# Loads and stores cut at partitions 112 and 48, and a new order of the first loads

## What is computed

```python
def step(m, rw):                       # over the 16 relations
    r, w_r = rw
    mask = jnp.where(etypes == r, 1.0, 0.0).astype(h.dtype)
    m = m + mask[:, None] * (h @ w_r)  # h = feat[src]
    return (m, None)
m, _ = jax.lax.scan(step, m0, (jnp.arange(n_rels), weight))
out = jax.ops.segment_sum(m, dst, num_segments=feat.shape[0])
...
x = _layernorm(x + out, axis=-1)
```

## Time and profile before

| what | value |
|---|---|
| median of 3 runs | 871.02 us (870.95 to 871.26) |
| span of the profiled execution | 870.6 us |
| instructions | 24502 |
| busy share | PE 79%, DVE 69%, POOL 68%, ACT 67% |
| software queue of the gathers | 19840 packets, 40.67 MB |
| hardware queue of SP | 9102 packets, 15.55 MB |
| hardware queue of ACT | 1316 packets, 1.06 MB |
| mean DMA rate | 66 GB/s over the span |

### The profile page before, as it was taken

One profiled execution on the slowest core, in us unless ns is written; L12 is line 12 of the kernel. 1 busy time (PEld: TensorE's weight loads), 2 busy tenths in 40 slices (PEclk: granted clock), 3 DMA queues, 4 the chain that ended last, 5 costly groups with the idle time before them and its releaser, 6 DMA issues.

```text
span 870.6 us, 24502 instructions
## 1 busy us (share of the span) xinstructions
PE 684.9 (79%) x8136; PEld 643.7 (74%) x8137; DVE 598.9 (69%) x2220; ACT 585.6 (67%) x1326; POOL 591.7 (68%) x634
## 2 busy tenths in 40 slices
PE   0004998888889888888898888889888888898894
PEld 0004888787878877887887788779877887798784
DVE  0146886767677776777678668766876687678754
ACT  1307777776777677677777777677777677777732
POOL 2005777777777777777777777777777777777760
PEclk9999899999999999999999999999999999999996
DMA  1022222222222222222222222222222222222211
GB/s 63 38 88 64 71 74 69 69 63 72 69 66 66 69 72 63 69 69 71 64 66 72 69 63 69 71 70 61 71 69 72 60 72 69 71 61 69 54 46 39
DMA packets 30272, 57.46 MB, mean 66 GB/s; under 512 B 11402, under 2 KB 19402, under 8 KB 30258
## 3 DMA queue, kind: packets, MB, share of 16 engines
q0 software_dynamic: 19840, 40.67, 19.6%
q1 hardware_dynamic: 9102, 15.55, 5.0%
q10 hardware_dynamic: 1316, 1.06, 0.4%
HBM read 54.84 MB, written 2.40 MB: 66 GB/s over the span
## 4 chain that ended last, share of the span: by engine, by line
POOL 61%; issue 25%; SPq 5%; DMA 4%; PE 2%; ACT 1%; DVE 1%; POOLq 0%; DVEq 0%; ACTq 0%
POOL rows L286 61%; DMA src_b<-in_src 4%; SPq L218 2%; SPq L217 2%; PE own L686 1%; ACT away L374 1%; DVE outT L571 1%; PE own L825 0%; PE rel L736 0%; PE agg L724 0%; POOLq L194 0%; DMA rows<-x_parts,gidx 0%; ACT pick L380 0%; DVE x_sb L600 0%; ACT krel L404 0%
## 5 line engine op out<-in xcount | busy, mean ns | idle before, releaser
L286 POOL DMA_INDIRECT rows<-x_parts,gidx x620 | 586.0, 945 | 244.0 <-issue 188.0
L686 PE MATMUL own<-xp,pick 125*128 125x192 bf16 x4650 | 412.8, 253 | 82.5 <-issue 74.6
L686 PEld LDWEIGHTS own<-xp,pick 125*128 125x128 bf16 x4650 | 397.2, 101 | 93.9 <-issue 83.9
L464 DVE TENSOR_SCALAR pick<-src_h,node 125x384 bf16<-125x384 f16 x1240 | 401.9, 402 | 8.4 <-ACT src_h L342 8.4
L528 DVE TENSOR_SCALAR onehot<-ramp,krel 128x112 bf16<-128x112 bf16 x806 | 149.4, 262 | 49.6 <-issue 49.6
L374 ACT ACTIVATE away<-src_h,node_neg 125x384 bf16<-125x384 f16 x310 | 169.6, 613 | 0.1
L380 ACT ACTIVATE pick<-away,one 125x384 bf16<-125x384 bf16 x310 | 163.0, 610 | 0.0
L724 PE MATMUL agg<-onehot,rows 128*128 128x112 bf16 x2418 | 139.8, 215 | 29.1 <-DMA rows<-x_parts,gidx 23.8
L724 PEld LDWEIGHTS agg<-onehot,rows 128*128 128x128 bf16 x2418 | 122.4, 99 | 48.2 <-issue 48.1
L388 ACT ACTIVATE rows<-own 128x192 bf16<-128x192 f32 x186 | 61.4, 330 | 138.9 <-PE own L686 131.7
L736 PE MATMUL rel<-aggT,w_pair 128*64 128x64 f32 x992 | 128.7, 298 | 0.0
(11 more groups left out here) (62 smaller groups left out, 72.6 us busy)
## 6 DMA issues: line engine op xcount, KB each, us to landing
src_b<-in_src SPq DMA_DIRECT2D x62, 187.5 KB
rows<-x_parts,gidx POOLq DMA_INDIRECT x620
x_parts<-xp SPq DMA_DIRECT2D x1, 812.5 KB
x_parts<-xp SPq DMA_DIRECT2D x1, 750.0 KB
out<-x_sb SPq DMA_DIRECT2D x2, 250.0 KB
x_sb<-in_x ACTq DMA_DIRECT2D x1, 406.2 KB
src_i<-in_src SPq DMA_DIRECT2D x1, 396.5 KB
dst_i<-in_dst SPq DMA_DIRECT2D x1, 396.5 KB
```

What stands on the lines that cost most here:

```text
L286: pool.indirect_dma_start(rows[:, u, j, :], None, x_parts, bass.IndirectOffsetOnAxis(ap=gidx[:, u, j:j + 1], axis=0)).then_inc(rows_in[u] ...
L464: v.tensor_scalar(pick[u][:, b, :], src_h[u][:, :, 0:CUTW[u]], node[:, b:b + 1], None, ALU.is_equal).then_inc(pick_ready[u], 1)
L686: return nc.tensor.matmul(own[h][:, 0:SPLIT * D], pick[u][:, b, h * P:(h + 1) * P], xp[:, b, 0:SPLIT, :].rearrange("p s d -> p (s d)"), st ...
```

## The change

- The loads of x, the stores to `x_parts` and the stores of the output take 112 and 13 partitions in two DMAs in place of 125 in one. The first 61 rows of `src`, `dst` and `etype` take 48 and 13 rows in two DMAs.
- `src_b` is 128 partitions high in place of 125, and its broadcast fills all of them; ACT reads the first 125.
- SP's order at the start is: `src`, `src_b` of the first half-turn, `dst`, `etype`, `src_b` of the second half-turn, the stores to `x_parts`, the two weight loads (which leave ACT's queue), `par_row`.
- The cast of `src` to float moves from ACT, behind its work on x, to the head of DVE's list.
- The semaphore counts follow.

```diff
+    NQ = 112
+    GQ = 48
+    PARTS = ((0, NQ), (NQ, NP))
...
-        src_b = [sb(f"src_b{u}", [NP, OWNW[u]], i32) for u in range(2)]
+        src_b = [sb(f"src_b{u}", [P, OWNW[u]], i32) for u in range(2)]
...
             def load(tile, a, s, pad_src):
-                sp.dma_start(tile[0:G - 1, :], a[0:(G - 1) * ROW].rearrange("(g e) -> g e", e=ROW)).then_inc(s, 16)
+                for g0, g1 in ((0, GQ), (GQ, G - 1)):
+                    sp.dma_start(tile[g0:g1, :], a[g0 * ROW:g1 * ROW].rearrange("(g e) -> g e", e=ROW)).then_inc(s, 16)
...
             load(src_i, src, src_in, row(src))
-
+            spread_sources(0, 0)
             load(dst_i, dst, dst_in, row(dst))
             sp.wait_ge(far_set, 1)
             load(et_i, etype, et_in, far_i[:, :])
+            spread_sources(0, 1)
...
-                sp.dma_start(pv[:, b0:b1, :], xp[:, b0:b1, :, :].rearrange("p b s d -> p b (s d)")).then_inc(parts_out, 16)
...
-                sp.dma_start(src_b[u][:, :], a.rearrange("(o e) -> o e", o=1).to_broadcast([NP, OWNW[u]])).then_inc(src_b_in[u], 16)
+                for p0, p1 in PARTS:
+                    sp.dma_start(pv[p0:p1, b0:b1, :], xp[p0:p1, b0:b1, :, :].rearrange("p b s d -> p b (s d)")).then_inc(parts_out, 16)
...
-            turn(0)
+            for q in range(2):
+                sp.dma_start(w_pair[q * D:(q + 1) * D, :, :],
+                             weight.rearrange("(q two) k d -> two k q d", two=2)[q]).then_inc(w_in, 16)
...
-                sp.dma_start(out.rearrange("(p b) d -> p b d", b=NB)[:, b0:b1, :], y[:, b0:b1, :]).then_inc(out_done, 16)
-            sp.wait_ge(out_done, 16 * YT)
+                for p0, p1 in PARTS:
+                    sp.dma_start(out.rearrange("(p b) d -> p b d", b=NB)[p0:p1, b0:b1, :], y[p0:p1, b0:b1, :]).then_inc(out_done, 16)
+            sp.wait_ge(out_done, 32 * YT)
...
-            pool.wait_ge(parts_out, 32)
+            pool.wait_ge(parts_out, 64)
...
-                act.dma_start(x_sb[:, b0:b1, :], x.rearrange("(p b) d -> p b d", b=NB)[:, b0:b1, :]).then_inc(x_in[n], 16)
-            for q in range(2):
-                act.dma_start(w_pair[q * D:(q + 1) * D, :, :],
-                              weight.rearrange("(q two) k d -> two k q d", two=2)[q]).then_inc(w_in, 16)
+                for p0, p1 in PARTS:
+                    act.dma_start(x_sb[p0:p1, b0:b1, :], x.rearrange("(p b) d -> p b d", b=NB)[p0:p1, b0:b1, :]).then_inc(x_in[n], 16)
...
-            act.wait_ge(src_in, 48)
-            act.activation(src_f[:, :], src_i[:, :], ACT.Copy).then_inc(src_cast, 1)
-
...
+            dve.wait_ge(src_in, 64)
+            v.tensor_copy(src_f[:, :], src_i[:, :]).then_inc(src_cast, 1)
             for n in range(2):
                 b0, b1 = XHALF[n], XHALF[n + 1]
                 dve.wait_ge(high_done, n + 1)
...
-            dve.wait_ge(dst_in, 48)
+            dve.wait_ge(dst_in, 64)
             step(v.tensor_copy(dst_f[:, :], dst_i[:, :]))
```

More of the change, by code:

```diff
@@ L221, in row, with spread_sources @@
                 return a[E - PAD:E].rearrange("(o e) -> o e", o=1)
+            def spread_sources(i, u):
+                if not is_first(i):
+                    sp.wait_ge(src_h_ready[u], i)
+                a = src[bass.ds(i * (2 * ROW) + u * ROW, OWNW[u])]
+                sp.dma_start(src_b[u][:, :], a.rearrange("(o e) -> o e", o=1).to_broadcast([P, OWNW[u]])).then_inc(src_b_in[u], 16)
             load(src_i, src, src_in, row(src))
+            spread_sources(0, 0)
             load(dst_i, dst, dst_in, row(dst))
@@ L274, in _ @@
             pool.memset(outT[:, :], 0.0).then_inc(out_zeroed, 1)
-            pool.wait_ge(x_in[0], 16)
+            pool.wait_ge(x_in[0], 32)
             pool.tensor_copy(xp[:, 0:XHALF[1], RP - 1, :], x_sb[:, 0:XHALF[1], :]).then_inc(again_done[0], 1)
-            pool.wait_ge(parts_out, 32)
+            pool.wait_ge(parts_out, 64)
             def fetch(i, u):
@@ L307, in _ @@
                 b0, b1 = XHALF[n], XHALF[n + 1]
-                act.dma_start(x_sb[:, b0:b1, :], x.rearrange("(p b) d -> p b d", b=NB)[:, b0:b1, :]).then_inc(x_in[n], 16)
-            for q in range(2):
-                act.dma_start(w_pair[q * D:(q + 1) * D, :, :],
-                              weight.rearrange("(q two) k d -> two k q d", two=2)[q]).then_inc(w_in, 16)
+                for p0, p1 in PARTS:
+                    act.dma_start(x_sb[p0:p1, b0:b1, :], x.rearrange("(p b) d -> p b d", b=NB)[p0:p1, b0:b1, :]).then_inc(x_in[n], 16)
             for n in range(2):
                 b0, b1 = XHALF[n], XHALF[n + 1]
-                act.wait_ge(x_in[n], 16)
+                act.wait_ge(x_in[n], 32)
                 act.activation(xp[:, b0:b1, 0, :], x_sb[:, b0:b1, :], ACT.Copy).then_inc(high_done, 1)
@@ L341, in narrow_sources @@
                     act.wait_ge(act_pick_ready[u], i)
-                act.activation(src_h[u][:, :, 0:CUTW[u]], src_b[u][:, :].rearrange("p (c w) -> p c w", c=CUT), ACT.Copy, bias=-float(MID)).then_inc(src_h_ready[u], 1)
+                act.activation(src_h[u][:, :, 0:CUTW[u]], src_b[u][0:NP, :].rearrange("p (c w) -> p c w", c=CUT), ACT.Copy, bias=-float(MID)).then_inc(src_h_ready[u], 1)
             def clear_agg(u):
@@ L393, in _ @@
             group_indices(0, 1)
-            act.wait_ge(et_in, 48)
+            act.wait_ge(et_in, 64)
             act.activation(et_f[:, :], et_i[:, :], ACT.Copy).then_inc(et_cast, 1)
```

## The result

The changed kernel takes 819.57 us (818.77 to 820.43, 4 runs) against 870.99 us (870.18 to 871.26, 4 runs): a ratio of 0.9406, 95% interval 0.9391 to 0.942. The profiled execution has a span of 817.0 us. The forecast was 813, range 808.5 to 821.

The account below looks back on a forecast made before the run. POOL's 620 gathers were taken to bound the middle, with start and end uncovered. 870.6 - 54.6 (earlier first gather) + 1.5 (collision) - 4.8 (end) = 812.7 us span, plus 0.4 gives 813.1, range 808.5 to 821.

Parts of the forecast that it names:

- the end: Output stores after DVE's last result: on 16 engines 2.6 us remain instead of 7.4, minus 4.8 us, bounds minus 3 and minus 5.5.
- the offset: Difference between the shown median and the profiled execution's span, taken as 0.4 us and added to 812.7 us.
- the collision: POOL's gathers stretched while DVE runs its two long float32 operations: plus 1.5 us, bounds 0 and 3.2.
- The loads: Start of the kernel: 16 engines at 410 GB/s bring x in at 6.7 us instead of before 24.00.
- rival 2: More engines bring no more rate, total stays at 144 GB/s: first gather at 31.6, 828 us; chance 0.08.
- From x to the store: ACT's second cast to DVE's last subtraction takes 3.70 us, low parts ready at 9.4 and 10.4; DVE's src cast costs nothing.
- The stores: Stores to x_parts move 1.6 million bytes at 410 GB/s in 3.9 us; first gather at 16.2, range 14 to 20.
- What is late next: Picks start 4.7 us behind the first gather; gather 21 keeps 5.2 us to spare, so POOL is not stopped.
- The middle: src_b copies of 128 rows on 16 engines beside the gathers cost nothing; bounds minus 0.5 and plus 2 us.
- 3: First gather early, but picks, krel or src_b over 5.2 us later than reckoned, POOL stands before gather 21: 818 us; chance 0.07.
- 4: Cut transfers run one after another as slowly as whole, SP blocks until 39.9, only w moves away: 869 us; chance 0.03.
- 5: Slower: src_b copies on 16 engines push POOL's gathers in all 62 half-turns, 871 to 929 us; chance 0.02.

Follow-up runs that it names:

- The groups of loads at the end: Changed kernel plus seven groups of six loads in flight together behind its output; the same bytes took 1.7 times as long into partitions 0 to 47 as 0 to 95.
- the two after: Against the kernel before: new order with only 125-row transfers cut, 1349.97 us, ratio 0.9888; all cuts in the old order, 1320.93 us, ratio 0.9676.

## Why the prediction was right, point by point

The sign, the main size and the mechanism held: the row count decides how many engines work, and this decides when POOL starts. All cuts in the old order brought the first gather from 70.76 to 21.99; the order alone brought nothing.

The median came 6.5 us above the forecast of 813.1: the first gather 5.1 later, the pace of the gathers 0.3, the end 1.1 better, the offset 2.2. The first gather, at 21.3, lies outside the range of 14 to 20 that this term had of its own. That the total stayed inside the range is in part luck: the collision and the end stayed far from their upper bounds, and so made room for it.

- **The loads: mis-sized.** "One engine at 26 GB/s makes 16 of them 410": x was to be in at 6.7 and was in at 10.3, so 3.6 us. Sixteen engines do not move sixteen times one. (Sixteen times 26 is 416, not 410, a slip of under 0.1 us.) The bound of 144 GB/s that made rival 2 was nearer for the sources (145 in 9 to 12) than the value taken. The groups of loads at the end show that loads into 48 and 13 neighbouring rows are held by the partitions they write. With x alone it was in at 6.2, so what is loaded beside it takes its share. The sentence on an HBM limit of 358 pointed the right way, but its 1.2 us were too few.
- **From x to the store: right.** 3.70 us were reckoned; 10.30 to 14.01 is 3.71. DVE's cast of `src` stood for `src` until 7.45 and kept the first remainder until 8.59, a place where the text saw up to 1 us; it cost none, as x's second half was later still.
- **The stores: mis-sized.** From the last part to the first gather 7.3 us in place of 5.8, the same in two orders (14.01 to 21.29, 9.96 to 17.29). They ran at 340 to 357 GB/s, so 1.6 MB need 4.7 us in place of 3.9, an estimate from 340; the other 0.7 us no run separates. With the loads this makes the 5.1 us.
- **`gidx`, w, `par_row`: right.** `gidx` was written by 15.57, 5.7 us ahead of the gather, and the weights were asked for at 39.38, long after their issues.
- **What is late next: right in kind.** The picks started 3.0 us behind the first gather, not 4.7, since the gather itself was late. POOL did not stand before gather 21, which ran at 48.13 with its `gidx` written by 38.96.
- **The collision: right.** Plus 1.5 us predicted; the first two gathers were 1.17 and 0.50 us longer, 1.7 in all, and first to last grew by 1.8. That the stretch moved to the fourth and fifth gather with DVE's operations shows the cause.
- **The middle: right.** Beyond the two stretched gathers first to last grew by 0.1 us, so 16 engines for `src_b` cost nothing where POOL bounds.
- **The end: right for the stores.** From DVE's last result to the end 2.8 us, predicted 2.6, before 7.4. The experiments show the cause: with the output stores whole it was 7.4 in the run of the order alone and 7.5 in that of the 61-row loads, with them cut 2.8 and 2.7 in the two after. Another 1.3 us came between the last gather and this result, 18.7 before and 17.4 here, and no step named them. The run with the stores before `etype` took 18.6 again. PE's granted clock fell to half, 1.2 GHz, 9.1 us behind the last gather before, 9.6 in that run and 10.6 here, and each time PE had stood for 0.7 us or more shortly before. That fits, but it was not tried, and this gain is not to be counted as the change's.
- **The offset: wrong.** The 0.4 us between median and span was taken as fixed. In the result and the runs behind it 1.8 to 2.0 us of every execution lie outside its span, with and without the change. The four spans here were 817.0 to 818.6, and the profiled one was the shortest. The median lies 2.6 above it, which adds 2.2 us to the miss.

Of the rivals, 3, 4 and 5 fell: POOL did not stand before gather 21, SP did not stand, and the gathers kept their 1.25 us. Rival 2 had the direction: the rate did not grow in step with the engines, but it did grow past 144.

## What to carry to other kernels

Read the DMA share beside every long wait: 0.06 or 0.31 in a stretch that waits for a transfer says that one or five of 16 engines work, and then the row count of that transfer is the first thing to look at. Do not reckon sixteen engines as sixteen times one: take a load at 150 to 250 GB/s and a store at 350, and less where few partitions are written or one row is read by all. Once the engines are all in use, what stands ahead of the critical transfer in the queues counts; here loading x first and holding back `etype`, `src_b` and the weights gave another 3.6 to 4.0 us.

## What the runs showed of the hardware

- A backlog on one engine stops the issuing queue: 14.5 to 20.1 us for one issue, in three kernels with 61-row loads; in the starts of those without, up to four issues together took at most 3.4 us.
- Loads in flight together: 150 GB/s into partitions 0 to 47, 254 into 0 to 95; one 1.5 KB row to 128 partitions 117, different rows 256.
- Two-tensor float32 operations of 1.88 us on DVE stretch an indirect gather beside them from 0.94 to up to 2.80 us, and the stretch moves with them.
- One program took 1318 us on a chip that granted PE 0.75 and 820 where it granted 0.97: POOL there waited 498.8 us for PE, and the change still took 49 us off (1367.28 to 1318.24).
